# Adding the causal triangle of an attention on VectorE, in the scores' PSUM bank, instead of with a matmul by the identity

## The reference, cut to what matters

```python
q = (x @ Wq).reshape(b, n, 16, 64).transpose(0, 2, 1, 3) * 64 ** -0.5
kv = x @ Wkv                                    # keys and values are the same, one head of 64
kv = concatenate([null_kv (1 row), kv], axis=1) # 1025 keys; the null key is column 0
sim = einsum('bhid,bjd->bhij', q, kv)
sim = where(triu(ones(n, n + 1), k=2), -max, sim)
out = einsum('bhij,bjd->bhid', softmax(sim), kv) ... @ Wout
```

## Time and profile before

| | us |
|---|---|
| median of three runs | 1517.54 |
| lowest and highest | 1509.4, 1518.91 |
| the profiled execution | 1519.78 |
| its span, first to last instruction | 1518.1 |

### The profile page before, as it was taken

The page is one execution under the profiler, slowest core; times in us unless marked ns, Lnnn a source line. Parts: engine busy times, 40 slices in busy tenths (PEclk is TensorE's granted clock), DMA queues, the critical chain, the costliest instruction groups (busy, mean ns, idle before and its releaser), DMA issues. The chain is left out here.

```text
span 1518.1 us, 28082 instructions
## 1 busy us (share of the span) xinstructions
PE 1300.0 (86%) x8368; PEld 539.0 (36%) x8368; DVE 1135.2 (75%) x1941; ACT 920.7 (61%) x1915; POOL 334.0 (22%) x552
## 2 busy tenths in 40 slices
PE   4699998888866999999988999999958999978895
PEld 2122221122124555555556555555631222212122
DVE  6899997799655677766644666677559999969985
ACT  3288887777735555555533555555425888867774
POOL 4200000110002434343422333343330000001000
PEclk9599999999867999999999999999977999989998
DMA  4511225322102321111110222220051212252211
GB/s 119 167 51 47 57 56 79 69 60 63 29 18 55 75 45 44 43 43 44 44 44 1 52 54 55 53 47 1 22 159 51 55 49 56 59 88 63 60 43 56
DMA packets 58910, 86.49 MB, mean 57 GB/s; under 512 B 22289, under 2 KB 32465, under 8 KB 58833
## 3 DMA queue, kind: packets, MB, share of 16 engines
q1 hardware_dynamic: 58832, 85.53, 24.1%
HBM read 37.79 MB, written 22.54 MB: 40 GB/s over the span
## 5 line engine op out<-in xcount | busy, mean ns | idle before, releaser
L917 DVE TENSOR_REDUCE neg_max<-ps 128x1 f32<-128x1024 f32 x512 | 600.8, 1217 | 76.7 <-PE ps L1158 67.8
L772 ACT ACTIVATE arena<-ps 128x512 f32<-128x512 f32 x1024 | 539.4, 602 | 189.7 <-PE ps L1173 186.9
L1173 PE MATMUL ps<-arena 50*128 50x512 bf16 x1024 | 321.9, 401 | 70.5 <-ACT arena L772 40.3
L993 DVE TENSOR_REDUCE a_neg_max<-ps 128x1 f32<-128x129 f32 (+7 forms) x256 | 193.2, 755 | 168.4 <-PE ps L1275 165.1
L1158 PE MATMUL ps<-arena 48*128 48x512 bf16 x1024 | 276.1, 408 | 26.9 <-DVE neg_max L917 24.8
L1187 PE MATMUL ps<-arena 128*32 128x512 f32 x2048 | 288.4, 637 | 2.8
L579 POOL TENSOR_SCALAR arena<-arena,a_rsum 128x128 f32<-128x128 f32 (+7 forms) x256 | 192.2, 751 | 374.9 <-DVE a_rsum L1001 363.8
L1275 PE MATMUL ps<-arena 128*128 128x512 bf16 (+4 forms) x1344 | 239.7, 305 | 9.5 <-ACT null_out L723 4.8
L1173 PEld LDWEIGHTS ps<-arena 50*128 50x128 bf16 x1024 | 78.5, 95 | 435.1 <-ACT arena L772 362.5
L686 ACT ACTIVATE arena<-ps,a_neg_max 128x129 f32<-128x129 f32 (+7 forms) x256 | 189.7, 742 | 60.6 <-DVE a_neg_max L993 58.5
L696 ACT ACTIVATE arena<-ps 128x128 f32<-128x128 f32 (+1 forms) x192 | 87.1, 454 | 206.4 <-PE ps L1288 205.1
(11 more groups left out here) (120 smaller groups left out, 804.3 us busy)
## 6 DMA issues: line engine op xcount, KB each, us to landing
arena<-stack_dram SPq DMA_DIRECT2D x128, 192.0 KB, 3.3
stack_dram<-arena SPq DMA_DIRECT2D x48, 256.0 KB, 3.8
arena<-arena SPq DMA_DIRECT2D x32, 384.0 KB, 4.4
o_dram<-arena SPq DMA_DIRECT2D x32, 256.0 KB, 2.1
arena<-arena SPq DMA_DIRECT2D x32, 256.0 KB, 5.0
arena<-o_dram SPq DMA_DIRECT2D x30, 256.0 KB, 4.6
arena<-max_dram SPq DMA_DIRECT2D x256, 1.0 KB
arena<-arena SPq DMA_DIRECT2D x32, 128.0 KB, 4.9
```

Source lines behind the costliest of these rows:

```text
L772: nc.scalar.activation(probs[:, t, :], ps[:, EXP_BANK[t], :], ACT.Exp, scale=F_SCALE).then_inc(probs_ready, 1)
L917: nc.vector.tensor_reduce(neg_max[:, g, t:t + 1], ps[:, bank:bank + 2, :].rearrange("p a b -> p (a b)"), AX, ALU.max, negate=True).then_in ...
L993: nc.vector.tensor_reduce(a_neg_max[:, t:t + 1], ps[:, S_BANK[t % 2]:S_BANK[t % 2] + (n + HALF - 1) // HALF, :].rearrange("p a b -> p (a b ...
L1173: ins = nc.tensor.matmul(ps[:, bank, :], stack[rows, g, 1, kt * P:(kt + 1) * P], stack[rows, g, 0, h * HALF:(h + 1) * HALF], start=True, s ...
```

## The change

The fourth pass of the scores goes, with `ident_bf`. VectorE adds `causal` to the last 128 columns of the scores, in place in PSUM, before its maximum, and the maximum waits for that through a new semaphore `a_masked`.

```diff
@@ gpsimd: constants
             nc.gpsimd.memset(causal[:, :], 0.0).then_inc(const_ready, 1)
-            nc.gpsimd.tensor_copy(ident_bf[:, :], ident[:, :]).then_inc(const_ready, 1)
             nc.gpsimd.memset(null_sel[:, :], 0.0).then_inc(const_ready, 1)
@@ vector: a_maximum
                 n = 1 + (STEPS[t][2] + 1) * P
+                scores = ps[:, S_BANK[t % 2]:S_BANK[t % 2] + (n + HALF - 1) // HALF, :].rearrange("p a b -> p (a b)")
                 dve.wait_ge(a_scores, NS * pg + t + 1)
-                nc.vector.tensor_reduce(a_neg_max[:, t:t + 1],
-                                        ps[:, S_BANK[t % 2]:S_BANK[t % 2] + (n + HALF - 1) // HALF, :].rearrange("p a b -> p (a b)")[:, 0:n],
-                                        AX, ALU.max, negate=True).then_inc(a_max, 1)
+                nc.vector.tensor_tensor(scores[:, n - P:n], scores[:, n - P:n], causal[:, :], ALU.add).then_inc(a_masked, 1)
+                dve.wait_ge(a_masked, NS * pg + t + 1)
+                nc.vector.tensor_reduce(a_neg_max[:, t:t + 1], scores[:, 0:n], AX, ALU.max, negate=True).then_inc(a_max, 1)
@@ vector: attention
+                dve.wait_ge(const_ready, 8)
@@ tensor: a_score_tile
-                    m0, m1 = max(c0, 1 + qt * P), c1
                     bank = S_BANK[t % 2] + c0 // HALF
                     passes = [(q_s[:, par, hh, k, cols], key[:, b, c0:c1], 0, c1 - c0) for k, key in enumerate((k_a, k_a, k_b))]
-                    if m1 > m0:
-                        passes.append((ident_bf[:, :], causal[:, m0 - 1 - qt * P:m1 - 1 - qt * P], m0 - c0, m1 - c0))
```

More of the change, by code:

```diff
@@ L91, in build @@
         null_out = sb("null_out", [AH, C])
-        ident_bf = sb("ident_bf", [P, P], BF16)
         causal = sb("causal", [P, P], BF16)
@@ L187, in build @@
         a_max = sem("a_max")
+        a_masked = sem("a_masked")
         a_exp = sem("a_exp")
@@ L466, in _ @@
             nc.gpsimd.memset(causal[:, :], 0.0).then_inc(const_ready, 1)
-            nc.gpsimd.tensor_copy(ident_bf[:, :], ident[:, :]).then_inc(const_ready, 1)
             nc.gpsimd.memset(null_sel[:, :], 0.0).then_inc(const_ready, 1)
-            pool.wait_ge(const_ready, 8)
+            pool.wait_ge(const_ready, 7)
             nc.gpsimd.affine_select(out=causal[:, :], in_=causal[:, :], compare_op=ALU.is_ge, fill=MASKED, base=0,
                                     pattern=[[-1, P]], channel_multiplier=1).then_inc(const_ready, 1)
-            pool.wait_ge(const_ready, 9)
+            pool.wait_ge(const_ready, 8)
             def split(f):
@@ L525, in ffn @@
                                               null_col[h * AD:(h + 1) * AD, :].broadcast_to([AD, PAIRS])).then_inc(const_ready, 1)
-                        pool.wait_ge(const_ready, 10 + h)
+                        pool.wait_ge(const_ready, 9 + h)
                 for b in range(B):
@@ L1329, in attention @@
                     keys(b)
-                pe.wait_ge(const_ready, 11)
+                pe.wait_ge(const_ready, 10)
                 pe.wait_ge(xnT_ready, 2 * 2 * B)
```

## The result

| | before | after |
|---|---|---|
| median of four runs each, us | 1518.22 | 1546.17 |
| lowest and highest, us | 1509.4, 1529.39 | 1535.77, 1548.54 |
| profiled execution, its span, us | 1519.78, 1518.1 | 1548.54, 1546.8 |
| a looped group in the middle, us | 36.00 | 38.16 |
| a group from written-out lists, us | 35.56 | 37.04 |

The change makes the kernel slower: ratio of the times 1.0167, 95% interval 1.0085 to 1.0249. The forecast was +35 us, the medians lie 28 apart.

The account below looks back on a forecast made before the run. VectorE's list was taken to bound steps 2 to 7 and 12 to 15, TensorE steps 8 to 11, 0 and 1. +2.26 us a group times 15.5 gave +35 us, a median of 1553 us, range 1537 to 1566.

Parts of the forecast that it names:

- The price of one addition, 0.28 + 0.04: VectorE, each step: addition's duration 0.28 plus 0.04 for the maximum's wait, 0.32 us; bounds 0.21 and 0.42.
- What TensorE gets back: TensorE's stream: each removed mask matmul returns 0.05 us, 20 of them some 1.0 us a group where TensorE bounds.
- Steps 2 to 7, +1.38: First stretch, VectorE's list: six additions, 1.92, less 0.05, 0.32 and 0.17, delay the products with the values by 1.38 us.
- Steps 8 to 11, -0.25: Middle stretch, TensorE bounds: additions of 8, 9, 10 vanish in VectorE's idle time; five masks give back 0.25 us.
- Steps 12 to 1, +1.28 - 0.1 and the mask at the end of it: Last stretch: four additions delay VectorE's copies by 1.28 us, less 0.1 idle before step 15's maximum and 0.05 mask.
- the second way through step 11: Step 11's addition lies on an equally long path: maximum of 11, its exponential, then the scores of step 13.
- The group, +2.26: Sum over one attention group: 1.38 - 0.25 + 1.28 - 0.1 - 0.05 = +2.26 us, ten of sixteen additions on the path.
- I count 15.5 groups: Attention's 16 groups counted as 15.5, since first and last lack part of their side work: +35 us in all.
- TensorE's waits for VectorE, "over 4": TensorE's waits for VectorE's copies and readings grow from 2.1 us a group to over 4.
- The trade works: Rival, whole attention: VectorE's 7.7 us of waiting absorbs 5.1 us of additions, TensorE keeps its saving; -16 us, chance 0.04.
- Nearly hidden: Rival, attention: additions cost as little as the low price and the rest slides; 0 to +15 us, chance 0.09.
- Serial: Rival, attention: all sixteen additions delay the next scores; +82 us, 1600, or +58 us if GpSimd holds additions; chance 0.12.

Follow-up runs that it names:

- both_free: Kernel before, mask matmuls kept, plus VectorE additions into an unread SBUF tile that the maximum doesn't wait for; looped group 37.30 us, whole time 1526.8 us.
- no_mask: Kernel before with no mask at all on the diagonal tile, neither matmul nor addition; looped group 35.47 us, whole time 1498.1 us.
- idle_11: Kernel before with VectorE's addition in steps 0, 1, 8, 9, 10 and 11 only, matmul elsewhere; looped group 35.74 us, whole time 1507.8 us.
- add_idle: Kernel before with VectorE's addition in steps 0, 1, 8, 9 and 10 only, matmul elsewhere; looped group 35.81 us, time ratio 0.9962.

## Why the prediction was right, and where its size was off

The sign, the mechanism and the range were right; the time was 7 us too high, and smaller misses in the sum partly cancelled. Step by step:

- **The price of one addition, 0.28 + 0.04.** Measured 0.295, and 0.33 from start to start in the mean. Right, and both_free shows that the wait belongs in it: without it the price is 0.21.
- **What TensorE gets back.** 0.05 us a mask, one at step 2, five in the middle and one later, made 0.35 a group. The runs show 0.39 and 0.53. What I had missed lies in the middle (0.34 in no_mask, where I had 0.25) and in steps 13 to 15 (0.08, where I had nothing).
- **Steps 2 to 7, +1.38.** Measured +1.31. The two terms that were taken off are in the trace: the product held by GpSimd fell from 0.94 to 0.60 (0.34, forecast 0.32), and the idle 0.25 ahead of the reading is gone. That place gave more than the 0.17 of the sum: the reading started 0.41 us after the product before it and starts 0.11 after it now, so 0.30.
- **Steps 8 to 11, -0.25.** Measured -0.20.
- **Steps 12 to 1, +1.28 - 0.1 and the mask at the end of it.** Measured +1.06, 0.07 less than the sum's 1.13. The place ahead of step 15's maximum gave 0.16, not 0.1: the scores were met 0.28 us after the product before (642.74 to 643.02) and are met 0.12 after it now. Of the second way through step 11 nothing shows: step 11 alone costs nothing (idle_11), and the parts without it already sum to more than the whole change.
- **The group, +2.26.** Measured +2.16 in the looped groups.
- **"I count 15.5 groups".** This is the term that failed, in its size. The group I had read was one of the eight looped ones. The other eight have lists without register instructions and so more idle time on VectorE (0.66 and 0.44 us at the two places where the sum took off 0.17 and 0.1), and the six steady ones of them pay 1.48 (the last two 1.41 and 1.35). Summed over the trace: eight looped groups 17.3 us, six written-out ones 8.7, the group with the turn between the batches 1.1, and the first group 2.1, in all 29.2 for the attention. (The 1.1 is uncertain, since that group's time follows the clock, see add_idle.) Outside of the attention the first layer was 7 us shorter and the third 6.5 longer, which cancels. That is luck, as far as the runs show: both go with TensorE's granted clock and not with the edits. Over the 13 profiled runs the time up to the attention's first maximum was 473.5 to 475.4 us with a mean clock of 0.89, or 465.8 to 468.4 with 0.91; behind the last maximum it was 461.0 and 461.3 us with 0.90 and 0.89, or 451.3 to 454.8 with 0.92 or 0.93.
- **TensorE's waits for VectorE, "over 4".** Measured 3.2. I had put the whole shift down to waits on VectorE. TensorE's time without a matmul grew by 2.5 us a group (36.0 - 33.79 to 38.17 - 33.46); 1.1 of it is shown as a wait of the matmuls for VectorE, 0.6 as one for ScalarE's exponential and 0.4 as one for GpSimd, which the same list of the kernel before doesn't have. ScalarE's own waits for the maximum grew from 3.8 to 7.4 us, so VectorE may have made these late too; that is not shown. The rest has no releaser in the rows that I read.

The rivals. "The trade works" fell for the whole change: a wait of 7.7 us on VectorE was no room for 5.1 us of work. But it holds for the five steps where the engine waits and nobody waits for it, which is add_idle. "Nearly hidden", up to +15 us, fell too: the medians lie 28 apart and the attention alone grew by 29. "Serial" fell at steps 8 to 11, where VectorE still waits 1.2 to 1.7 us after the change. The addition isn't held by GpSimd in any of its 256 instances, unlike the one-column product.

Open: why groups with VectorE's list written out beside a looping TensorE take 35.35 us, and groups written out on every engine 35.56. No run takes TensorE's loop alone away. Nor was the addition tried behind the maximum, on scores that only the exponential would read; no run shows what it would cost or gain there.

## What to carry to other kernels

Ask of a trade between two engines not which is busier over the span, but which of the moved instructions stand in a list that somebody waits for: here ten of sixteen did, and moving the other six gains (0.26 us a group). Count a dependent VectorE instruction at its duration plus the gap of a waiting pair, read from the trace of before. And when one period is multiplied out, first see whether all periods are issued alike: a looped list and a written-out one have different slack, and the same edit cost 2.16 us in the one and 1.48 in the other.

## What the runs showed of the hardware that was not expected

- The wait of a row maximum for the addition of 128 columns before it costs 0.12 us (0.33 against 0.21 from start to start), 1.18 us over a group.
- Register instructions in a looped VectorE list are not free. One between a waiting pair costs 0.10 us, and writing the list out gave 0.65 us a group in the kernel before and 1.34 in the kernel after.
- Adding in place in PSUM costs next to nothing more than writing a bf16 tile in SBUF: 295 ns against 287.
- VectorE's one-column product with both inputs in SBUF lasted 0.94 and 0.60 us beside GpSimd's subtraction, in place of 0.16, and ended with it: the subtraction in the looped group of the kernel before took from 621.04 to 622.20, the product from 621.27 to 622.21. The addition with one input in SBUF never did such a thing (at most 300 ns in 256). The Trainium skill, "SBUF — State Buffer", Who interferes with whom, says that VectorE, outside of its 2-port modes, contends with a GpSimd instruction that reads SBUF if it has two inputs in SBUF itself, and not with one. These instructions agree with that. Not all do: six products of the kernel before that start 0.05 or 0.06 us into a GpSimd product (L579) took 0.16 us all the same; GpSimd's spans are rough, so this may be their error.
- The stretches outside the steady groups vary by 7 to 10 us from run to run, and their length goes with the granted clock of TensorE: 60.2 to 61.5 us at a mean of 1.00 and 66.4 to 67.2 at 0.92 for the one between the batches.
